# Order of three pairs of steps inside the second half of each group of tiles, in the layer stage of an AdaLN kernel

## The chip, the cores and the metric

One core of one Trainium2 chip runs the whole program. The metric is the time of one execution on the device in microseconds; the kernel before takes 2164.86 us (median of 3 runs, 2164.37 to 2165.76). The core has TensorE (PE in the rows; its weight loads are PEld), VectorE (DVE), ScalarE (ACT), GpSimd (POOL) and the queue SyncE (SP), which issues the DMAs. Each engine works through its own list of instructions in the order in which the program wrote them, and waits on semaphores.

## The reference

The input x has 4 sequences of 1024 tokens with 256 features. A small modulation network gives shift, scale and gate rows. First comes a normalised full attention with 4 heads, added to x through a gate. Then the input of the second part is normalised and modulated, goes through two layers, and is added through a second gate. One such layer is, cut to what matters here:

```python
h = shift_token(x)                       # half of the features come from the token before
q, k, v = split(h @ wqkv, 3)             # 8 heads of 64
q = l2norm(q) * qs;  k = l2norm(k) * ksc
q = q * cos * scale + rotate_half(q) * sin * scale      # k likewise, with 1/scale
o = local_attention(q, k, v)             # windows of 128 tokens: own one and the one before
x = x + o @ wo
h = layernorm(shift_token(x)) * lg + lb
a, g = split(h @ w1 + b1, 2)             # hidden size 682
x = x + (a * gelu(g)) @ w2 + b2
```

Everything is float32. Matrix products on TensorE are made of three products of rounded operands (hi*hi, hi*lo, lo*hi), so each operand has a "hi" copy, which ScalarE makes, and a "lo" remainder, which VectorE makes.

## The kernel before, in words

A set-up block and the first attention (`attention_block`) take about the first 700 us. The change is in `layers_block`, which handles both layers. It walks over 64 units of 128 tokens (32 a layer) in 16 groups of four (`QUAD`), g = 0 to 15, with a prologue g = -1. In group g, `first` is the group's first unit and `following` the first unit of the next group. Each engine has a hand-written list for a group, and the lists of all engines have the same skeleton.

First come 12 rounds r = 0 to 11 (`EARLY`) of attention: scores, softmax, transposes of the probabilities, value products. Then come 16 slots k = 0 to 15 (`SLOTS`). They hold the end of the attention; the q, k, v products of the group ahead (`qkv`, slots 0 to 11); the feed-forward part of the present group, 12 hidden units m = 0 to 11 of 114 or 113 features by 256 tokens; and the preparation of q and k of the group ahead. Six hidden units belong to one pair of token units. The text calls them unit 0 to unit 11.

What a hidden unit m passes through: `hidden` on PE in slot m + 4 makes the two products g and a in two of the banks A0 to A3. `gelu` (ACT L1420, slot m + 4) makes the gelu of g. `up_out` (DVE L1638, slot m + 5) multiplies it with a. `u_split` on ACT (L1427) makes the hi copy, `u_split` on DVE (L1644, slot m + 6) the lo remainder; its two inputs are both in SBUF. `outputs` on PE (L1281 to L1283, six matmuls) adds the unit to the layer's output in bank O or P; `outputs(0)` stands in slot 10, `outputs(5)` in slot 15, and units 6 to 11 follow in rounds 0 and 2 of the next group. `y_out` (DVE L1651) closes the six units of a pair.

What q and k of a unit n of the group ahead pass through: copies out of the bank to SBUF (ACT L1355); `squares` (ACT L1365); `sums` (DVE L1545); `trig`, three products with a table on POOL (two of L1802, one of L1807), which waits for the squares to have been summed; `norms` on DVE (lines 1551 to 1558 and `rsqrt`, 89 to 94); `rotated` (DVE L1563, L1565); `qk_transpose` on PE (L1210, eight transposes into the two banks T0 and T1); `qk_out` on ACT (L1372 for q, L1374 for k). There are only the banks T0 and T1 for these, so the transposes of the second unit wait until `qk_out` has emptied T0 of the first one's q. `sums` of the third unit is in slot 11 and of the fourth in slot 13, each with its `trig` on POOL one slot later.

`x_bias` (POOL L1820) adds the bias b2 to the residual, in slots 1, 5 and 7; its result is read by `y_out` at the end of the slots.

Of the kernel before, what the change touches and what calls it, by code (L numbers as in the profile page):

```python
# [1038 lines left out]
def layers_block(nc, io, scratch, out, ident, cols, share, early):  # L1039
# [3 lines left out]
    with ExitStack() as ctx:  # L1043
# [141 lines left out]
        def _(eng):  # L1185
# [68 lines left out]
            def x_transpose(n):  # L1254
                ps = fill(w, "x_t", n, "T")
                w.wait_ge(xn_ready, n + 1)
                for k in range(KC):
                    last = eng.transpose(ps[:, P * k:P * k + P], xn[:, n % 2, P * k:P * k + P], ident[:, :])
                last.then_inc(done["x_t"][0], 1)
# [27 lines left out]
            for g in range(-1, GROUPS + 1):  # L1287
                first, following, m0 = QUAD * g, QUAD * (g + 1), HC * g
                if g == GROUPS:
                    for j in range(NC):  # L1290
                        outputs(HC * (g - 1) + NC + j)
                    break
                if g >= 0:
                    for r in range(0, EARLY, 2):
                        if r >= 4:
                            p_transpose(*head(first, r - 4)), p_transpose(*head(first, r - 3))
                        scores(*head(first, r)), scores(*head(first, r + 1))
                        if g >= 1:
                            for j in OUT_AT.get(r, ()):
                                outputs(HC * (g - 1) + NC + j)  # L1300
                        elif r in (0, 2):
                            qkv(*LATE_V[r // 2])
                        if r in (4, 6):
                            qk_transpose(first + 2 + (r - 4) // 2)
                        if r == 8:
                            project(first)
                        if r == 10 and following < UNITS:
                            h_transpose(following)
                        if r >= 4:
                            values(*head(first, r - 4)), values(*head(first, r - 3))  # L1310
                for k in range(SLOTS):
                    ahead = following < UNITS
                    r = EARLY + 2 * k
                    if g >= 0 and k < 4:
                        p_transpose(*head(first, r - 4)), p_transpose(*head(first, r - 3))
                    if g >= 0 and k < 2:
                        scores(*head(first, r)), scores(*head(first, r + 1))
                    if k < HC and ahead and (following + k // 3, k % 3) not in LATE_V:
                        qkv(following + k // 3, k % 3)
                    if g >= 0:  # L1320
                        if k in (0, 4, 6):
                            project(first + (1, 0, 2, 3)[k // 2])
                        if k == 3:
                            x_transpose(first), x_transpose(first + 1)
                        if k == 0 and ahead:
                            h_transpose(following + 1)
                        if k < 4:
                            values(*head(first, r - 4)), values(*head(first, r - 3))
                    if k in (4, 7) and ahead:
                        h_transpose(following + 1 + k // 3)  # L1330
                    if k >= 4 and g >= 0:
                        hidden(m0 + k - 4)
                    if k == 9 and g >= 0:
                        x_transpose(first + 2), x_transpose(first + 3)
                    if k in (10, 11) and ahead:
                        qk_transpose(following + k - 10)
                    if k >= 10 and g >= 0:
                        outputs(m0 + k - 10)

        @block.scalar  # L1340
        def _(eng):
# [20 lines left out]
            def squares(n):  # L1362
                w.wait_ge(qk_ready, 2 * n + 2)
                w.wait_ge(t2_used, n - 1)
                eng.activation(t2[:, n % 2], qk[:, n % 3], ACT.Square).then_inc(sq_ready, 1)  # L1365
# [107 lines left out]
            for g in range(-1, GROUPS):  # L1473
                first, following, m0 = QUAD * g, QUAD * (g + 1), HC * g
                ahead = following < UNITS
                if g >= 0:
                    for r in range(EARLY):
                        if r == 8:
                            o_out(first)
                        if r >= 4 and r % 2 == 0:  # L1480
                            pt_out(*head(first, r - 4)), pt_out(*head(first, r - 3))
                        exps(*head(first, r))
                        if g == 0 and r in (1, 3):
                            qkv_out(*LATE_V[r // 2])
                        if r in (4, 6):
                            qk_out(first + 2 + (r - 4) // 2)
                        if r == 10 and ahead:
                            h_out(following)
                        if g == GL - 1:
                            for i in W_Q.get(r, ()):  # L1490
                                piece_q(i)
                        if g == GL:
                            for i in W_O.get(r, ()):
                                piece_o(i)
                            for i in W_1.get(r, ()):
                                piece_1(i)
                for k in range(SLOTS):
                    r = EARLY + 2 * k
                    if g >= 0:
                        if k in (0, 2, 4):  # L1500
                            o_out(first + 1 + k // 2)
                        if k < 4:
                            pt_out(*head(first, r - 4)), pt_out(*head(first, r - 3))
                    if k < HC and ahead and (following + k // 3, k % 3) not in LATE_V:
                        qkv_out(following + k // 3, k % 3)
                    if g >= 0:
                        if k < 2:
                            exps(*head(first, r)), exps(*head(first, r + 1))
                        if g == GL and k in (7, 9, 11):
                            piece_2((k - 7) // 2)  # L1510
                        if k == 3:
                            f_out(first), f_out(first + 1)
                    if (k in (4, 7) or k == 0 and g >= 0) and ahead:
                        h_out(following + 1 + k // 3)
                    if k in (2, 5, 10, 12) and ahead:
                        squares(following + k // 3 - k // 10)
                    if k >= 4 and g >= 0:
                        gelu(m0 + k - 4)
                    if k >= 5 and g >= 0:
                        u_split(m0 + k - 5)  # L1520
                    if k == 9 and g >= 0:
                        f_out(first + 2), f_out(first + 3)
                    if k in (11, 12) and ahead:
                        qk_out(following + k - 11)
                    if g == -1 and k == 3:
                        first_w2_wo()
                    if g == -1 and k == 6:
                        first_w1()
                if g >= 0:
                    u_split(m0 + HC - 1)  # L1530
# [250 lines left out]
        def _(eng):  # L1781
# [57 lines left out]
            def piece_2(i):  # L1839
                w.wait_ge(w2_hi, 2 + i + 1)  # L1840
                n = CS[2 * i]
                eng.tensor_tensor(w2[1][0:n, 2 * i:2 * i + 2, :].rearrange("p c n -> p (c n)"), AT_2[i][0:n, :],
                                  w2[0][0:n, 2 * i:2 * i + 2, :].rearrange("p c n -> p (c n)").bitcast(F32), ALU.subtract).then_inc(w2_ready, 1)
# [3 lines left out]
            for g in range(-1, GROUPS + 1):  # L1847
                first, following, m0 = QUAD * g, QUAD * (g + 1), HC * g
                ahead = following < UNITS
# [19 lines left out]
                for k in range(SLOTS):  # L1869
                    r = EARLY + 2 * k  # L1870
                    if k < 3 and g >= 0:
                        probabilities(*head(first, r - 2)), probabilities(*head(first, r - 1))
                    if g == GL and k in (7, 9, 11):
                        piece_2((k - 7) // 2)
                    if k in (1, 5, 7) and g >= 0:
                        x_bias(first + 1 + (k - 1) // 3)
                    if k in (4, 7, 12, 14) and ahead and (g >= 0 or k < 14):
                        trig(following + {4: 0, 7: 1, 12: 2, 14: 3}[k])
                if g >= 0:
                    finish(first), finish(first + 1)  # L1880

# [220 lines left out]
```

## Time and profile before

| | |
|---|---|
| median of 3 runs | 2164.86 us |
| the profiled execution's own time | 2162.62 us |
| its span | 2160.8 us |
| PE busy | 1869.9 us (87%) |
| PEld busy | 1395.4 us (65%) |
| DVE busy | 1529.1 us (71%) |
| ACT busy | 1186.4 us (55%) |
| POOL busy | 984.6 us (46%) |
| mean granted clock of TensorE | 0.953 |

The busy times overlap, and PE's is the time in which some matmul was in flight, not its speed. The 16 DMA engines were busy for about a tenth of the span. In the chain that ended last PE has 32% of the span, DVE 20% and ACT 8%. The layer stage begins at about 700 us. One group in the middle of it runs from 1170.22 to 1258.42 us, which is 88.2 us; the rows below are from this group unless they say otherwise.

### The profile page before, as it was taken

To read this page: it belongs to the slowest core of one execution; us is meant where nothing else is said; L and a number is where in the kernel's file an instruction comes from. 1 tells how busy PE (TensorE), PEld (TensorE's weight loads), DVE (VectorE), ACT (ScalarE), POOL (GpSimd) and SP (SyncE) were. 2 spreads that over 40 slices of the span, in tenths; PEclk is the share of its full clock that TensorE was granted. 3 is DMA by queue.
4 is the path that set the end of the run, shared out by engine and by line. 5 is a ranking of instruction groups with operands and counts; after the bars stand their busy time and mean duration, and the time that the engine had idled before them with its cause. 6 is when DMAs were issued, how large, how long until landed. Compare 5 with 4: busy or idle time off the path is not lost.

```text
span 2160.8 us, 36526 instructions
## 1 busy us (share of the span) xinstructions
PE 1869.9 (87%) x12941; PEld 1395.4 (65%) x12941; DVE 1529.1 (71%) x3736; ACT 1186.4 (55%) x2717; POOL 984.6 (46%) x781
## 2 busy tenths in 40 slices
PE   5568999999984899899999999888899998998996
PEld 3444444444443587777777877767787777877776
DVE  2668888676756686867867768586776867768674
ACT  0545545534343656656566565665656566565662
POOL 0324454647473545334444444543545445454451
PEclk7669999999996899999999999999999999999999
DMA  4000000101212000000000001111101000010100
GB/s 141 28 27 28 1 25 11 42 25 42 89 54 88 8 21 22 19 12 24 21 17 19 12 25 35 51 51 28 33 16 30 27 27 26 18 30 25 29 19 23
DMA packets 83407, 68.58 MB, mean 32 GB/s; under 512 B 10853, under 2 KB 79509, under 8 KB 83225
## 3 DMA queue, kind: packets, MB, share of 16 engines
q1 hardware_dynamic: 83224, 66.25, 9.9%
q8 instruction: 103, 1.69, 0.3%
q14 instruction: 80, 0.65, 0.1%
HBM read 45.22 MB, written 16.81 MB: 29 GB/s over the span
## 4 chain that ended last, share of the span: by engine, by line
PE 32%; DVE 20%; ACT 8%; issue 7%; DMA 1%; POOL 1%; DVEq 0%; ACTq 0%; SPq 0%; POOLq 0%
ACT share_x L1383 4%; PE bank_A L260 3%; PE bank_A L262 3%; PE bank_A L261 3%; PE bank_P L260 3%; PE bank_A L1220 3%; DVE l_t L1563 2%; PE bank_O L1243 2%; PE bank_P L262 2%; DVE share_x L1579 2%; PE bank_P L261 2%; PE bank_T L1231 2%; DVE l_u_lo L1644 2%; PE bank_T L1210 2%; PE bank_T L260 1%
## 5 line engine op out<-in xcount | busy, mean ns | idle before, releaser
L1814 POOL TENSOR_TENSOR share_x<-share_x,l_rinv 128x512 f32<-128x512 f32 (+1 forms) x256 | 249.9, 997 | 343.0 <-DVE l_rinv L1587 342.7
L1802 POOL TENSOR_TENSOR l_t<-share_qk,l_tab 128x512 f32<-128x512 f32 x128 | 176.0, 1396 | 318.7 <-DVE l_ss L1545 313.3
L1383 ACT ACTIVATE share_x<-share_x,l_nb 128x256 f32<-128x256 f32 (+1 forms) x512 | 248.2, 487 | 80.6 <-DVE l_nb L1579 80.4
L260 PE MATMUL bank_A<-l_f_hi,l_w_hi 128*114 128x256 f32 (+1 forms) x768 | 220.0, 286 | 6.2 <-DVE l_f_lo L1624 5.0
L262 PE MATMUL bank_A<-l_f_hi,l_w_lo 128*114 128x256 f32 (+1 forms) x768 | 216.1, 281 | 0.0
L261 PE MATMUL bank_A<-l_f_lo,l_w_hi 128*114 128x256 f32 (+1 forms) x768 | 215.9, 281 | 0.0
L1579 DVE CUSTOM_DVE_ANT_0 share_x<-bank_A,share_scr 128x256 f32<-128x256 f32 (+1 forms) x512 | 177.2, 401 | 42.7 <-PE bank_A L1220 42.5
L645 ACT ACTIVATE pr<-ps_S 128x1024 f32<-128x1024 f32 x128 | 130.6, 1022 | 124.7 <-PE ps_S L539 124.0
L1644 DVE TENSOR_TENSOR l_u_lo<-l_up,l_u_hi 114x256 fp32r<-114x256 f32 (+1 forms) x192 | 196.8, 1031 | 0.1
L1231 PE MATMUL bank_T<-ident,share_x 128*128 128x128 f32 x960 | 150.5, 287 | 53.1 <-POOL share_x L1814 40.1
L760 DVE TENSOR_REDUCE mxr<-ps_M 128x2 f32<-128x1024 f32 x128 | 154.9, 1210 | 36.3 <-PE ps_M L550 35.6
L895 POOL TENSOR_TENSOR acc<-acc,pr 128x1024 f32<-128x1024 f32 x64 | 156.2, 2441 | 53.0 <-ACT pr L645 48.7
L1231 PEld LDWEIGHTS bank_T<-ident,share_x 128*128 128x128 f32 x960 | 102.5, 142 | 95.8 <-issue 48.6
L1807 POOL TENSOR_TENSOR l_t<-share_qk,l_tab 128x1024 f32<-128x1024 f32 x64 | 157.7, 2464 | 0.0
L260 PE MATMUL bank_P<-l_wqkv_hi,l_h_hi 128*128 128x512 f32 x368 | 155.8, 423 | 1.5 <-ACT l_vt L1360 1.0
L1394 ACT COPY share_qk<-bank_T 128x512 f32<-128x512 f32 (+1 forms) x256 | 133.0, 557 | 42.9 <-PE bank_T L1231 40.9
L1420 ACT ACTIVATE share_x<-bank_A,cols 114x256 f32<-114x256 f32 (+1 forms) x192 | 90.8, 473 | 108.4 <-PE bank_A L262 101.9
L1355 ACT COPY share_qk<-bank_P 128x512 f32<-128x512 f32 x122 | 71.6, 587 | 141.7 <-PE bank_P L262 141.7
L1220 PE MATMUL bank_A<-l_kt,share_x 64*128 64x256 f32 (+1 forms) x1024 | 146.9, 403 | 0.7 <-DVE l_nb L1579 0.2
L1243 PE MATMUL bank_O<-share_qk,l_vt 128*64 128x128 f32 x1920 | 139.7, 283 | 8.0 <-DVE l_o_lo L1591 8.0
L261 PE MATMUL bank_P<-l_wqkv_lo,l_h_hi 128*128 128x512 f32 x368 | 146.3, 398 | 0.0
L260 PEld LDWEIGHTS bank_A<-l_f_hi,l_w_hi 128*114 128x114 f32 (+1 forms) x768 | 136.0, 177 | 15.7 <-issue 12.5
(269 smaller groups left out, 5098.8 us busy)
## 6 DMA issues: line engine op xcount, KB each, us to landing
l_xs<-x_layers SPq DMA_DIRECT2D x64, 128.0 KB, 2.5
share_x<-in_x SPq DMA_DIRECT2D x8, 512.0 KB, 3.8
base_rows<-share_x SPq DMA_DIRECT2D x16, 256.0 KB, 2.1
x_layers<-share_x SPq DMA_DIRECT2D x16, 256.0 KB, 2.1
l_xs<-x_layers SPq DMA_DIRECT2D x64, 64.0 KB, 2.1
x_layers<-l_yb SPq DMA_DIRECT2D x32, 128.0 KB, 1.8
share_m<-base_rows SPq DMA_DIRECT2D x32, 128.0 KB, 2.7
out<-l_yb SPq DMA_DIRECT2D x32, 128.0 KB, 1.7
```

What stands on the lines that cost most here:

```text
L260: pe.matmul(out, a_hi, b_hi, start=(start and k == 0), stop=False)
L261: pe.matmul(out, a_hi, b_lo, start=False, stop=False)
L262: last = pe.matmul(out, a_lo, b_hi, start=False, stop=(stop and k == n - 1))
L1220: last = eng.matmul(halves[e][:, 0:P * windows(n)], qt[rows, n % QUAD, c, :], kt[rows, key_slots(n), c, :], start=True, stop=True)
L1231: last = eng.transpose(ps[:, q:q + P], sm[:, R % SS, e, P * v:P * v + P], ident[:, :])
L1243: last = eng.matmul(banks["O"][HD * e:HD * e + HD, P * c:P * c + P], vt[:, s, q:q + HD], pt[:, R % 2, 2 * e + v, :], start=(v == 0), stop= ...
L1383: eng.activation(row, row, ACT.Exp, bias=nb[:, R % SS, e:e + 1], scale=-1.0, accum_out=rsum[:, R % SS, e:e + 1]).then_inc(ex_ready, 1)
L1579: eng.tensor_tensor_reduce(sm[:, R % SS, e, 0:P * windows(n)], ps[:, 0:P * windows(n)], keep, 1.0, 3.0e38, ALU.add, ALU.min, nb[:, R % SS, ...
L1644: eng.tensor_tensor(u_lo[0:CS[j], m % US, :], up[0:CS[j], m % 3, :], u_hi[0:CS[j], m % US, :].bitcast(F32), ALU.subtract).then_inc(u_ready, 1)
L1802: eng.tensor_tensor(dst[:, :, :, lo:lo + H2], src[:, :, :, hi:hi + H2], table[:, :, 1, lo:lo + H2].unsqueeze(2).to_broadcast([P, 2, LH, H2 ...
L1807: eng.tensor_tensor(t1[:, n % 2].rearrange("p (a h) d -> p a h d", a=2), src, table[:, :, 0, :].unsqueeze(2).to_broadcast([P, 2, LH, HD]), ...
L1814: eng.tensor_tensor(row, row, rinv[:, R % SS, :].unsqueeze(2).to_broadcast([P, 2, P * windows(n)]), ALU.mult).then_inc(pn_ready, 1)
```

## The change

Three edits, all in the slots. PE: in slots 10 and 11 `outputs(m0 + k - 10)` stands in front of `qk_transpose(following + k - 10)`, no longer behind it. ACT: in slots 11 and 12 `qk_out(following + k - 11)` stands in front of `gelu(m0 + k - 4)` and `u_split(m0 + k - 5)`. POOL: `trig` stands in front of `x_bias`; the two meet in slot 7 only, with `trig(following + 1)` and `x_bias(first + 3)`. DVE's and SP's lists are the same. No instruction is added or removed.

```diff
@@ PE
                     if k == 9 and g >= 0:
                         x_transpose(first + 2), x_transpose(first + 3)
+                    if k >= 10 and g >= 0:
+                        outputs(m0 + k - 10)
                     if k in (10, 11) and ahead:
                         qk_transpose(following + k - 10)
-                    if k >= 10 and g >= 0:
-                        outputs(m0 + k - 10)
@@ ACT
                     if k in (2, 5, 10, 12) and ahead:
                         squares(following + k // 3 - k // 10)
+                    if k in (11, 12) and ahead:
+                        qk_out(following + k - 11)
                     if k >= 4 and g >= 0:
                         gelu(m0 + k - 4)
                     if k >= 5 and g >= 0:
                         u_split(m0 + k - 5)
                     if k == 9 and g >= 0:
                         f_out(first + 2), f_out(first + 3)
-                    if k in (11, 12) and ahead:
-                        qk_out(following + k - 11)
@@ POOL
+                    if k in (4, 7, 12, 14) and ahead and (g >= 0 or k < 14):
+                        trig(following + {4: 0, 7: 1, 12: 2, 14: 3}[k])
                     if k in (1, 5, 7) and g >= 0:
                         x_bias(first + 1 + (k - 1) // 3)
-                    if k in (4, 7, 12, 14) and ahead and (g >= 0 or k < 14):
-                        trig(following + {4: 0, 7: 1, 12: 2, 14: 3}[k])
```

## Rows read from the trace of the kernel before

**Rows 1.** Busy time by engine between two moments: stretch, length, engines (instructions), clock, DMA.
```profile
1223.40:1245.47 22.07, 20.59 (x159) 18.93 (x160) 19.43 (x27) 11.11 (x24) 10.35 (x6) 1.00 0.00 1
```

**Rows 2.** Timeline of PE: start, length, instruction, count, idle time before and what ended it.
```profile
1227.95 1.09 PE L1210 MATMUL bank_T<-ident,l_t 128*128 128x128 f32 x8 [0.66 <-DVE l_t L1565]
1228.79 0.37 PE L1281 MATMUL bank_O<-l_w_hi,l_u_hi 114*128 114x256 f32 x1
...
1229.59 0.40 PE L260 MATMUL bank_P<-l_wqkv_hi,l_h_hi 128*128 128x512 f32 x1
...
1230.99 0.28 PE L260 MATMUL bank_A<-l_f_hi,l_w_hi 128*114 128x256 f32 x1
...
1233.21 1.15 PE L1210 MATMUL bank_T<-ident,l_t 128*128 128x128 f32 x8 [0.64 <-ACT share_x L1372]
1234.11 0.36 PE L1281 MATMUL bank_O<-l_w_hi,l_u_hi 114*128 114x256 f32 x1
...
1234.90 0.28 PE L260 MATMUL bank_A<-l_f_hi,l_w_hi 128*114 128x256 f32 x1
```

**Rows 3.** Timeline of ACT in the same slots.
```profile
1231.19 0.59 ACT L1360 COPY l_vt<-bank_P 128x512 f32<-128x512 f32 x1 [2.47 <-PE bank_P L262]
1231.91 0.47 ACT L1420 ACTIVATE share_x<-bank_A,cols 114x256 f32<-114x256 f32 x1
...
1232.57 0.59 ACT L1372 COPY share_x<-bank_T 128x512 f32<-128x512 f32 x1
...
1233.53 1.08 ACT L1365 ACTIVATE l_t<-share_qk 128x1024 f32<-128x1024 f32 x1
1235.81 0.48 ACT L1420 ACTIVATE share_x<-bank_A,cols 114x256 f32<-114x256 f32 x1 [1.20 <-PE bank_A L262]
```

**Rows 4.** Timeline of DVE, slots 8 to 15.
```profile
1217.24 2.25 DVE L1644 TENSOR_TENSOR l_u_lo<-l_up,l_u_hi 114x256 fp32r<-114x256 f32 x1
...
1220.07 0.18 DVE L1551 TENSOR_SCALAR l_ss<-l_ss 128x32 f32<-128x32 f32 x1
...
1232.79 0.47 DVE L1638 SCALAR_TENSOR_TENSOR l_up<-bank_A,cols,share_x 114x256 f32<-114x256 f32 x1
...
1236.52 0.48 DVE L1638 SCALAR_TENSOR_TENSOR l_up<-bank_A,cols,share_x 114x256 f32<-114x256 f32 x1 [1.93 <-PE bank_A L262]
1236.92 1.46 DVE L1644 TENSOR_TENSOR l_u_lo<-l_up,l_u_hi 114x256 fp32r<-114x256 f32 x1
...
1243.31 2.23 DVE L1644 TENSOR_TENSOR l_u_lo<-l_up,l_u_hi 113x256 fp32r<-113x256 f32 x2
1245.47 0.68 DVE L1651 TENSOR_TENSOR l_yb<-bank_O,l_yb 128x512 f32<-128x512 f32 x1
```

**Rows 5.** Timeline of POOL, slots 7 to 15.
```profile
1212.91 0.73 POOL L1820 TENSOR_TENSOR l_yb<-l_xs,share_scr 128x256 f32<-128x256 f32 x1 [4.16 <-DVE l_xs L1597]
1214.10 2.73 POOL L1802 TENSOR_TENSOR l_t<-share_qk,l_tab 128x512 f32<-128x512 f32 x2 [0.46 <-DVE l_ss L1545]
...
1233.01 2.73 POOL L1802 TENSOR_TENSOR l_t<-share_qk,l_tab 128x512 f32<-128x512 f32 x2 [13.81 <-DVE l_ss L1545]
1235.71 2.39 POOL L1807 TENSOR_TENSOR l_t<-share_qk,l_tab 128x1024 f32<-128x1024 f32 x1
1239.66 2.74 POOL L1802 TENSOR_TENSOR l_t<-share_qk,l_tab 128x512 f32<-128x512 f32 x2 [1.56 <-DVE l_ss L1545]
1242.36 2.56 POOL L1807 TENSOR_TENSOR l_t<-share_qk,l_tab 128x1024 f32<-128x1024 f32 x1
```

**Rows 6.** All instructions of line 1644: count, shortest, median and longest in ns.
```profile
L1644 DVE TENSOR_TENSOR l_u_lo<-l_up,l_u_hi x192: 407/1120/2248, 766.8 to 2149.5; 114x256 fp32r<-114x256 f32 x128, 113x256 fp32r<-113x256 f32 x64
```

**Rows 7.** Timeline of DVE in the first group of layer two.
```profile
1496.63 1.32 DVE L1554 TENSOR_SCALAR l_ss<-l_mv 128x2 f32<-128x2 f32 x1
```

**Rows 8.** Timeline of PE: the wait of slot 11 in groups 0 and 14.
```profile
788.36 0.82 PE L1210 MATMUL bank_T<-ident,l_t 128*128 128x128 f32 x5 [0.64 <-ACT share_x L1372]
...
2058.57 0.66 PE L1210 MATMUL bank_T<-ident,l_t 128*128 128x128 f32 x4 [0.64 <-ACT share_x L1372]
```

## The prediction

> **What bounds the kernel now.** I read the page first, then the chain of waits, then the timelines of all four engines over one group, because the page's shares are means over stages with different limits. PE is busy longest, but in the stretch that the change touches no engine is busy all the time: of 22.07 us PE has 20.59, DVE 19.43, ACT 11.11, POOL 10.35, at a granted clock of 1.00, the level of 2.4 GHz [rows 1]. So the question is who waits for whom. The reader is to see two holes on PE, 0.66 us ahead of the transposes of the first unit (they wait for DVE's `rotated`) and 0.64 us ahead of those of the second (they wait until ACT has emptied bank T0) [rows 2]. On DVE the hole is in front of unit 8: `up_out` starts at 1236.52 after 1.93 us idle, waiting for PE's product a [rows 4]. From the end of `norms` to there DVE goes almost without a pause, so what PE gains before counts only up to this hole. Behind it stands a second resource, which no view names as a releaser. DVE's `u_split` takes 0.41 us at its shortest and 1.12 at the median [rows 6]. The one of 1236.92 lasts 1.46 us and ends at 1238.38, just after POOL's L1807 ends at 1235.71 + 2.39 = 1238.10. The pair of 1243.31 ends at 1245.54, 0.62 after POOL's L1807 ends at 1242.36 + 2.56 = 1244.92, and `y_out` follows [rows 4, 5]. I read this as an exclusion: a `u_split` started during a POOL product waits for the end of that one instruction. POOL is delayed in turn by some 0.16 where DVE waits at a boundary (2.56 against 2.39) [rows 5]. Then the end of the group hangs on POOL: `y_out` comes when the fourth `trig` is over, this started at 1239.66, and it waited 1.56 us for `sums` [rows 5], which stands on DVE behind the `u_split` of 1236.92.
>
> The Trainium skill says the same in the page "SBUF — State Buffer", section "Who interferes with whom": a DVE instruction with two SBUF inputs and a GpSimd instruction that reads SBUF exclude each other, and the later one waits until the earlier is finished. The lengths of rows 4 to 6 agree. The rule speaks against a plain reading of this change: time won on PE in the slots is worth nothing unless it moves a boundary of POOL.
>
> **Edit 1, PE.** `outputs(0)` costs 1229.59 - 1228.79 = 0.80, of which about 0.1 is the slow first matmul behind transposes (0.37 against 0.28) [rows 2]; ahead of the transposes it costs 0.70. The hole of 0.66 is counted from the end of the last matmul in flight; a matmul of 0.28 takes its turn in 0.12, so the room is 0.82. It fits, the transposes stay at 1227.95, and what follows them starts 0.70 earlier: the v product is ready for ACT at 1231.19 - 0.70 = 1230.49, unit 7's `hidden` starts at 1230.99 - 0.70 = 1230.29. That takes 1.42 (1230.99 to 1233.21 - 0.64 - 0.16), then `outputs(1)` 0.70: PE is at the second transposes at 1232.41, against 1233.21.
>
> **Edit 2, ACT.** ACT's turns: two copies take 0.96 (1232.57 to 1233.53), one 0.48; `gelu` with the hi copy 0.66 (1231.91 to 1232.57); `squares` 0.96, estimated as its 1.08 less the 0.11 by which a copy of 0.59 outlasts its turn [rows 3]. New order: v copy 1230.49, `qk_out` of the first unit 1230.97, so T0 is free at about 1231.6, before PE asks; the second hole is gone. `gelu(7)` at 1231.93 instead of 1231.91 [rows 3], harmless, since DVE takes unit 7 at 1232.79 only [rows 4]. `squares` at 1232.59, second `qk_out` 1233.55, `gelu(8)` at 1234.51 instead of 1235.81. PE: second transposes 1232.41 to 1233.31 (0.90, rows 2), `hidden` of unit 8 at 1233.3 instead of 1234.90. In the trace `up_out` of unit 8 starts 1.62 after it (1236.52 - 1234.90), with the slow first matmul 1.70: 1235.0. After `gelu(8)` (0.48 and some 0.1 of signalling, an estimate) it is 1235.1. So `up_out` of unit 8 moves from 1236.52 to 1235.1, and `u_split` asks for its turn 0.40 later, at 1235.5.
>
> **The step that decides.** POOL's boundary between L1802 and L1807 is at 1235.71 [rows 5]. 1235.5 is before it by 0.2. The remainder then runs in the boundary, ends near 1236.0 instead of 1238.38, `sums` ends near 1237.2, and the fourth `trig` waits no more for it: it starts when the third ends, 1238.10 + 0.16 = 1238.27, instead of 1239.66. That is 1.39 us. `trig` itself lasts as long as before (5.26, from 1239.66 to 1244.92), DVE's last remainders and `y_out` follow it 1.39 earlier; PE, which is 1.6 ahead, isn't late. Everything in the next group starts from `y_out`, the scores' minima and POOL's release, so the gain should stay. `up_out` and PE find their banks free, as `up_out` runs two units ahead of the reuse.
>
> **Edit 3, POOL.** The `trig` of slot 7 starts no earlier: with `x_bias` done it still waits 0.46 for `sums` [rows 5]. `x_bias` moves from 1212.91, inside a wait of 4.16 for the residual, to behind L1807, at 1219.2; its reader `y_out` is 25 us away. Price: it holds the port while DVE is about to begin `norms`. With 0.73 + 0.16 it ends at 1220.1, `norms` starts at 1220.07 [rows 4]: 0.05. Below: 0, if such a small instruction isn't held up; against that, one of 128x2 elements took 1.32 under POOL's work [rows 7]. Above: 0.73, if `x_bias` gets its turn before the waiting `u_split` of 1217.24 [rows 4] and shifts the whole chain. I take 0.05, since at the boundary of 1238.10 and at that of 1244.92 the waiting DVE was next.
>
> **Sum.** Groups 0 to 14 have a group ahead. In 14 of them the timelines repeat within 0.05 us; the holes of groups 0 and 14 are again 0.64 [rows 8]. 14 x 1.39 = 19.5. Group 8, where layer two begins, has other spacings, with 0 to 1.4 possible; I take 0.7. `x_bias` gives back 15 x 0.05 = 0.8. In sum 19.4 us. The profiled execution took 2162.62 (span 2160.8), 2.2 under the median: it would come to 2143.2, the median from 2164.86 to 2145.5.
>
> **Rivals.** *The boundary is missed.* If `u_split` asks after 1235.71, it waits until 1238.10, as now, and `sums`, the fourth `trig` and `y_out` stay where they are; PE's 1.6 us end in a longer wait. For it speaks that the margin is 0.2 us at the end of a dozen steps; against it, that every step is a row of this group and that the groups don't scatter. It would hit all groups or none: 2164.86 + 0.8 = 2165.6, the change does nothing.
>
> *`x_bias` goes first, the boundary is met.* 15 x 0.73 = 11.0 us are paid, 20.2 won: 2155.7.
>
> *`x_bias` goes first, and nothing is won.* The mechanism is its port turn in front of the remainder of 1217.24; this pushes `norms`, the layer norm and `rotated` by 0.73 in each group. It decides as soon as the gain behind is under 0.73, so with a missed boundary: 2164.86 + 11.0 = 2175.9, slower.
>
> **Numbers.** Boundary met as forecast 0.62; met with the price of `x_bias` 0.10; missed 0.18; missed and paid 0.10. Less than 0.2% (4.3 us) can't be told from no change. So faster 0.72, same 0.18, slower 0.10. The first case alone would lie between 2142 (group 8 in full, no price) and 2149 (1.1 a group). The range goes from 2142 to 2167, which takes in the first three cases.
>
> **What would show it.** In the profile after: no idle ahead of the L1210 of slots 10 and 11 beyond 0.1 us; L1420 of unit 8 before the L1807 of the third `trig`, and the L1644 behind it under 0.6 us instead of 1.46; the fourth `trig`'s L1802 without a wait for L1545; `y_out` 1.4 us earlier counted from `norms`; L1820 of slot 7 directly behind L1807 and L1551 at most 0.1 later. The prediction is wrong if that L1644 still lasts over a microsecond up to the end of L1807, or if the shortened slots come back as a longer wait in the rounds of the next group.

## The result: 2140.32 us, and the profile after

The changed kernel takes 2140.32 us (median of 6 runs, 2139.02 to 2145.55), the kernel before, with three more runs beside it, 2162.61 (2157.89 to 2165.76). The ratio is 0.9904, 95% interval 0.9886 to 0.9922, which is 20.8 us (17 to 25); the two medians are 22.3 us apart. The direction, the size and the mechanism of the forecast (19.4 us) hold. The time itself lies 1.7 us under the range that was stated: the executions of either kernel fall into two clusters some 5 us apart, for which neither the sum nor its range had a term. Two executions of the kernel before that were taken beside experiments, of 2568.49 and 3446.82 us, are left out of every comparison as slow ones.

The page of the changed kernel, busy times and the chain:

```profile
span 2139.0 us, 36526 instructions
PE 1871.9 (88%) x12941; PEld 1400.3 (65%) x12941; DVE 1505.0 (70%) x3736; ACT 1185.0 (55%) x2717; POOL 989.3 (46%) x781
PE 34%; DVE 19%; issue 7%; ACT 7%; DMA 1%; POOL 1%; DVEq 0%; SPq 0%; ACTq 0%; POOLq 0%
```

The reader is to see DVE: the same 3736 instructions are busy 24.1 us less (1529.1 before). They don't do less, they are held up less: L1644 alone has 172.5 us in all instead of 196.8. This total is no measure of the gain, though. With the PE edit alone, which below gives the same time, L1644 has 182.8 us. PE is as busy as before, in a span 21.8 shorter.

The timelines show the same group as the rows of before (group 5). It is best counted from the group's last layer-norm statistics, DVE's L1602, at 1219.41 before and 1208.26 after, which is a shift of 11.15. First PE; this answers [rows 2]:

```profile
1216.00 0.28 PE L1281 MATMUL bank_O<-l_w_hi,l_u_hi 114*128 114x256 f32 x1
...
1216.80 1.09 PE L1210 MATMUL bank_T<-ident,l_t 128*128 128x128 f32 x8
1217.65 0.48 PE L260 MATMUL bank_P<-l_wqkv_hi,l_h_hi 128*128 128x512 f32 x1
...
1221.25 1.04 PE L1210 MATMUL bank_T<-ident,l_t 128*128 128x128 f32 x8
1222.05 0.36 PE L260 MATMUL bank_A<-l_f_hi,l_w_hi 128*114 128x256 f32 x1
```

Both holes are gone. The first transposes start where they did (8.54 after L1602 in both), the product behind them 0.8 earlier, unit 8's `hidden` (1222.05) 1.7 earlier. Then ACT, which answers [rows 3]:

```profile
1219.33 0.59 ACT L1360 COPY l_vt<-bank_P 128x512 f32<-128x512 f32 x1 [1.75 <-PE bank_P L262]
1219.82 0.59 ACT L1372 COPY share_x<-bank_T 128x512 f32<-128x512 f32 x1
...
1223.34 0.52 ACT L1420 ACTIVATE share_x<-bank_A,cols 114x256 f32<-114x256 f32 x1
```

`gelu(8)` stands 15.08 after L1602; 15.10 was forecast, and 16.40 was the kernel before. The stage that decides is on DVE and POOL, which answer [rows 4, 5]:

```profile
1222.04 1.41 DVE L1644 TENSOR_TENSOR l_u_lo<-l_up,l_u_hi 114x256 fp32r<-114x256 f32 x1
1223.95 0.48 DVE L1638 SCALAR_TENSOR_TENSOR l_up<-bank_A,cols,share_x 114x256 f32<-114x256 f32 x1 [0.50 <-PE bank_A L262]
1224.35 0.54 DVE L1644 TENSOR_TENSOR l_u_lo<-l_up,l_u_hi 114x256 fp32r<-114x256 f32 x1
1224.81 1.21 DVE L1545 TENSOR_REDUCE l_ss<-l_t 128x16 f32<-128x1024 f32 x1
...
1232.91 0.68 DVE L1651 TENSOR_TENSOR l_yb<-bank_O,l_yb 128x512 f32<-128x512 f32 x1
```

```profile
1208.02 0.92 POOL L1820 TENSOR_TENSOR l_yb<-l_xs,share_scr 128x256 f32<-128x256 f32 x1
1221.87 2.74 POOL L1802 TENSOR_TENSOR l_t<-share_qk,l_tab 128x512 f32<-128x512 f32 x2 [12.93 <-DVE l_ss L1545]
1224.57 2.58 POOL L1807 TENSOR_TENSOR l_t<-share_qk,l_tab 128x1024 f32<-128x1024 f32 x1
1227.12 2.92 POOL L1802 TENSOR_TENSOR l_t<-share_qk,l_tab 128x512 f32<-128x512 f32 x2
1229.98 2.39 POOL L1807 TENSOR_TENSOR l_t<-share_qk,l_tab 128x1024 f32<-128x1024 f32 x1
```

DVE's L1644 behind unit 8 starts at 1224.35, before POOL's boundary at 1224.57. It ends after 0.54 us instead of 1.46; POOL's L1807 takes 2.58 instead of 2.39 and shows the other side of the same meeting. The fourth `trig` has no wait for `sums` any more. `y_out` comes 24.65 after L1602 instead of 26.06: 1.41 us, against 1.39 forecast.

Where the difference sits in the whole program can be read from the first and last start of L1602, which runs four times a group (one row each, before and after):

```profile
L1602 DVE BATCH_NORM_STATS2 l_st<-l_xs x64: 412/427/430, 743.5 to 2129.0; 128x6 f32<-128x256 f32 x64
```

```profile
L1602 DVE BATCH_NORM_STATS2 l_st<-l_xs x64: 412/426/430, 739.5 to 2106.6; 128x6 f32<-128x256 f32 x64
```

Of the 22.4 us at the last start, 4.0 are there at the first already, ahead of the first changed step. Between them it is 18.4: this stage takes 1385.5 us before and 1367.1 after. Both parts are taken up below.

### The profile page after: what moved, and what is told of

Read it like the earlier page. It is cut to its first block, busy times and chain, and to the rows that moved or that the text cites. A ratio compares the mean times of both kernels' runs of the same rounds, so it can differ in the third digit from the quotient of the medians.

```text
span 2139.0 us, 36526 instructions
## 1 busy us (share of the span) xinstructions
PE 1871.9 (88%) x12941; PEld 1400.3 (65%) x12941; DVE 1505.0 (70%) x3736; ACT 1185.0 (55%) x2717; POOL 989.3 (46%) x781
## 4 chain that ended last, share of the span: by engine, by line
PE 34%; DVE 19%; issue 7%; ACT 7%; DMA 1%; POOL 1%; DVEq 0%; SPq 0%; ACTq 0%; POOLq 0%
ACT share_x L1383 4%; PE bank_A L260 4%; PE bank_A L262 3%; PE bank_A L261 3%; PE bank_P L260 3%; PE bank_A L1220 3%; PE bank_P L262 2%; PE bank_P L261 2%; DVE share_x L1579 2%; PE bank_O L1243 2%; DVE l_u_lo L1644 2%; PE bank_T L1231 2%; DVE l_t L1563 2%; PE bank_T L1210 2%; PE bank_T L260 1%
## 5 line engine op out<-in xcount | busy, mean ns | idle before, releaser
L1802 POOL TENSOR_TENSOR l_t<-share_qk,l_tab 128x512 f32<-128x512 f32 x128 | 178.8, 1419 | 351.8 <-DVE l_ss L1545 346.4
L895 POOL TENSOR_TENSOR acc<-acc,pr 128x1024 f32<-128x1024 f32 x64 | 156.1, 2439 | 48.2 <-ACT pr L645 43.7
L1644 DVE TENSOR_TENSOR l_u_lo<-l_up,l_u_hi 114x256 fp32r<-114x256 f32 (+1 forms) x192 | 172.5, 905 | 0.1
L1807 POOL TENSOR_TENSOR l_t<-share_qk,l_tab 128x1024 f32<-128x1024 f32 x64 | 157.5, 2461 | 0.0
L260 PEld LDWEIGHTS bank_A<-l_f_hi,l_w_hi 128*114 128x114 f32 (+1 forms) x768 | 136.2, 177 | 15.7 <-issue 12.5
L262 PE MATMUL bank_P<-l_wqkv_hi,l_h_lo 128*128 128x512 f32 x368 | 145.9, 397 | 0.0
```

The source lines that it names most:

```text
L260: pe.matmul(out, a_hi, b_hi, start=(start and k == 0), stop=False)
L262: last = pe.matmul(out, a_lo, b_hi, start=False, stop=(stop and k == n - 1))
L1644: eng.tensor_tensor(u_lo[0:CS[j], m % US, :], up[0:CS[j], m % 3, :], u_hi[0:CS[j], m % US, :].bitcast(F32), ALU.subtract).then_inc(u_ready, 1)
L1802: eng.tensor_tensor(dst[:, :, :, lo:lo + H2], src[:, :, :, hi:hi + H2], table[:, :, 1, lo:lo + H2].unsqueeze(2).to_broadcast([P, 2, LH, H2 ...
L1807: eng.tensor_tensor(t1[:, n % 2].rearrange("p (a h) d -> p a h d", a=2), src, table[:, :, 0, :].unsqueeze(2).to_broadcast([P, 2, LH, HD]), ...
```

## The experiments

**One edit at a time.** Each is the kernel before with one of the three hunks of the diff. PE alone:

```diff
+                    if k >= 10 and g >= 0:
+                        outputs(m0 + k - 10)
                     if k in (10, 11) and ahead:
                         qk_transpose(following + k - 10)
-                    if k >= 10 and g >= 0:
-                        outputs(m0 + k - 10)
```

> The kernel before with the PE edit alone (outputs in front of qk_transpose). Boundary theory: outputs(0) fills the first hole, v is ready 0.7 us earlier, gelu(7) comes at 1231.2 and qk_out behind it frees T0 at 1232.5, just when PE asks; unit 8's up_out at 1235.1, its u_split in POOL's boundary of 1235.7, and the group is 1.4 us shorter, nearly as with all three edits: 17 to 21 us faster in all, 2141 to 2146. Rival (all three edits are needed, each gives its part): about a third to a half, 7 to 11 us.

Measured: 2141.98 us, ratio to before 0.9898 (0.988 to 0.9916). That is the whole gain, to within what the runs tell, and the stage from first to last L1602 takes 1367.1 us, as with all three edits. In its timeline L1644 behind unit 8 again has 0.54 us, and POOL's boundary comes 0.22 us after its start:

```profile
1222.26 0.49 DVE L1638 SCALAR_TENSOR_TENSOR l_up<-bank_A,cols,share_x 114x256 f32<-114x256 f32 x1 [0.50 <-PE bank_A L262]
1222.66 0.54 DVE L1644 TENSOR_TENSOR l_u_lo<-l_up,l_u_hi 114x256 fp32r<-114x256 f32 x1
```

```profile
1222.88 2.58 POOL L1807 TENSOR_TENSOR l_t<-share_qk,l_tab 128x1024 f32<-128x1024 f32 x1
```

ACT alone, `qk_out` in front of `gelu` and `u_split`:

```diff
+                    if k in (11, 12) and ahead:
+                        qk_out(following + k - 11)
                     if k >= 4 and g >= 0:
                         gelu(m0 + k - 4)
...
-                    if k in (11, 12) and ahead:
-                        qk_out(following + k - 11)
```

> The kernel before with the ACT edit alone (qk_out in front of gelu and u_split). Boundary theory: the second hole of PE closes (hidden of unit 8 starts 0.76 us earlier), but up_out of unit 8 comes at 1235.8 and its u_split asks at 1236.2, after POOL's boundary of 1235.7; so it waits to 1238.1 as before and the time does not change: 0 to 2 us. Rival (time won on PE counts as such): 0.76 us in each of 14 groups, 10.6 us faster.

Measured: 2164.40 us, ratio 1.0006 (0.9996 to 1.0016). The hole of slot 11 closes and `up_out` of unit 8 comes 0.73 us earlier in the group, yet L1644 misses the boundary of 1235.90 and just waits longer:

```profile
1235.98 0.48 DVE L1638 SCALAR_TENSOR_TENSOR l_up<-bank_A,cols,share_x 114x256 f32<-114x256 f32 x1 [1.20 <-PE bank_A L262]
1236.38 2.20 DVE L1644 TENSOR_TENSOR l_u_lo<-l_up,l_u_hi 114x256 fp32r<-114x256 f32 x1
```

```profile
1233.19 2.74 POOL L1802 TENSOR_TENSOR l_t<-share_qk,l_tab 128x512 f32<-128x512 f32 x2 [13.81 <-DVE l_ss L1545]
1235.90 2.40 POOL L1807 TENSOR_TENSOR l_t<-share_qk,l_tab 128x1024 f32<-128x1024 f32 x1
```

Half of what the full change wins ahead of this `up_out` (0.73 us of 1.42) is worth nothing here. That refutes the rival by which PE time counts as such, and it is the missed boundary of the prediction's first rival, seen on the chip.

POOL alone:

```diff
+                    if k in (4, 7, 12, 14) and ahead and (g >= 0 or k < 14):
+                        trig(following + {4: 0, 7: 1, 12: 2, 14: 3}[k])
                     if k in (1, 5, 7) and g >= 0:
                         x_bias(first + 1 + (k - 1) // 3)
-                    if k in (4, 7, 12, 14) and ahead and (g >= 0 or k < 14):
-                        trig(following + {4: 0, 7: 1, 12: 2, 14: 3}[k])
```

> The kernel before with the POOL edit alone (trig in front of x_bias in slot 7). Boundary theory: x_bias sits behind the third product of trig and is over before norms starts: no change, within 1 us. Rival (x_bias holds up norms): up to 0.7 us in 15 groups, 11 us slower.

Measured: 2164.83 us, ratio 0.9995 (0.9984 to 1.0006). Nothing, in either direction. That speaks against both rivals of the prediction in which `x_bias` is paid for: each charges 11.0 us for this edit, and the interval allows 1.3 us of slowing at most.

**One instruction on either side of the boundary.** The sharpest test adds work to the changed kernel. In front of `u_split`:

```diff
+        idle = sb("idle", [P, 6])
...
+                    if k == 13 and ahead and g >= 0:
+                        eng.bn_stats(idle[:, :], b2[:, 0, :])
                     if k >= 6 and g >= 0:
                         u_split(m0 + k - 6)
```

> The changed kernel with one more instruction on DVE in each group: a bn_stats over constants (128x256, 0.41 us, result unused), in slot 13 between up_out of unit 8 and the u_split behind it. In the changed kernel that u_split starts 0.22 us before POOL's boundary (16.09 against 16.31, counted from the group's last L1602). Boundary theory: it now asks at 16.5, waits for L1807 to end at 18.7, sums and the fourth trig come 1.4 us later, and the whole gain of the change is lost in 14 groups: 20 us slower than the changed kernel, about 2160 to 2165. Rival (no exclusion, plain work on DVE): at most 0.4 us in 15 groups, 6 us, or nothing, since DVE has idle time there.

Measured: 2164.38 us, ratio to the kernel before 0.9995 (0.9984 to 1.0006). An instruction of 0.42 us has undone a gain of 20. L1645 here is L1644, one line further down. It starts at 1231.76, 0.14 us behind POOL's boundary of 1231.62:

```profile
1231.03 0.48 DVE L1639 SCALAR_TENSOR_TENSOR l_up<-bank_A,cols,share_x 114x256 f32<-114x256 f32 x1 [0.52 <-PE bank_A L262]
1231.43 0.42 DVE L1747 BATCH_NORM_STATS2 l_idle<-share_scr 128x6 f32<-128x256 f32 x1
1231.76 2.53 DVE L1645 TENSOR_TENSOR l_u_lo<-l_up,l_u_hi 114x256 fp32r<-114x256 f32 x1
```

```profile
1231.62 2.39 POOL L1810 TENSOR_TENSOR l_t<-share_qk,l_tab 128x1024 f32<-128x1024 f32 x1
1235.57 2.73 POOL L1805 TENSOR_TENSOR l_t<-share_qk,l_tab 128x512 f32<-128x512 f32 x2 [1.55 <-DVE l_ss L1546]
```

The lines L1805 and L1810 are the old L1802 and L1807, and the wait for `sums` is back (1.55). The same instruction behind `u_split`:

```diff
                     if k >= 6 and g >= 0:
                         u_split(m0 + k - 6)
+                    if k == 13 and ahead and g >= 0:
+                        eng.bn_stats(idle[:, :], b2[:, 0, :])
```

> The same additional bn_stats, but behind that u_split, in front of sums of the fourth unit. Boundary theory: u_split still gets the boundary, sums ends at 18.2 instead of 17.8 (counted from the group's last L1602), and POOL is busy until 18.86 anyway: nothing is lost, as fast as the changed kernel, 2139 to 2146. Rival (plain work): the same loss as with the instruction in front.

Measured: 2144.22 us, ratio to before 0.9907 (0.989 to 0.9924). It costs nothing that the four runs can tell from the changed kernel; a few us aren't excluded, since in its profiled execution the stage from first to last L1602 takes 1370.4 instead of 1367.1 (2.6 us of it in group 6, 1.3 in group 8, 1.2 less in group 14). The two kernels with the additional instruction have the same instructions and differ by 0.9%.

```profile
1227.88 0.51 DVE L1645 TENSOR_TENSOR l_u_lo<-l_up,l_u_hi 114x256 fp32r<-114x256 f32 x1
1228.32 0.41 DVE L1749 BATCH_NORM_STATS2 l_idle<-share_scr 128x6 f32<-128x256 f32 x1
```

```profile
1228.07 2.59 POOL L1810 TENSOR_TENSOR l_t<-share_qk,l_tab 128x1024 f32<-128x1024 f32 x1
```

**`sums` moved ahead, in the kernel before.** DVE's list alone, slot 13:

```diff
+                    if k == 13 and ahead and g >= 0:
+                        sums(following + 3)
                     if k >= 6 and g >= 0:
                         u_split(m0 + k - 6)
...
-                    if k in (3, 6, 11, 13) and ahead:
+                    if k in (3, 6, 11, 13) and ahead and (k < 13 or g < 0):
                         sums(following + k // 3 - 1)
```

> The kernel before, PE, ACT and POOL as they were; only DVE's list is changed: in slot 13 sums(following + 3) stands in front of u_split of unit 7. If the group hangs on the fourth trig waiting for sums behind a blocked u_split, this gives the same gain with the holes of PE still there: sums ends at 1238.0, trig starts at 1238.1 instead of 1239.66, 1.4 us in 14 groups, 18 to 22 us faster (unless the last hidden units of PE, which stay where they were, become the later side: up_out of unit 11 at 1242.9 still allows 1.4). Rival (the gain comes from the holes on PE): 0 to 2 us.

Measured: 2152.34 us, ratio 0.9946 (0.9931 to 0.9962): 11.7 us, a good half of what was expected. The direction tells that the fourth `trig` is on the path even with both holes of PE still there. The size was misjudged. With `trig` early and PE late, another `u_split` starts 0.15 us behind the boundary of the long product (L1809, the old L1807): it lasts 2.52 us, and unit 11's `up_out`, expected at 1242.9 in the time of the rows of before (23.50 after L1602), comes 24.20 after it. `y_out` waits for that and comes 25.48 after L1602, 0.58 us earlier than in the kernel before instead of 1.4.

```profile
1237.16 2.52 DVE L1644 TENSOR_TENSOR l_u_lo<-l_up,l_u_hi 114x256 fp32r<-114x256 f32 x1
1239.61 0.47 DVE L1638 SCALAR_TENSOR_TENSOR l_up<-bank_A,cols,share_x 113x256 f32<-113x256 f32 x1
```

```profile
1237.01 2.39 POOL L1809 TENSOR_TENSOR l_t<-share_qk,l_tab 128x1024 f32<-128x1024 f32 x1
```

**A version that beats both.** If blocked remainders hold up the group's end, they needn't stand there. The changed kernel, DVE's list:

```diff
                 if g >= 0:
                     up_out(m0 + HC - 1)
-                    u_split(m0 + HC - 2), u_split(m0 + HC - 1)
+                    if not ahead:
+                        u_split(m0 + HC - 2), u_split(m0 + HC - 1)
                     y_out(2 * g)
...  (rounds of the next group)
                         minima(*head(first, r))
+                        if r == 1 and g >= 1:
+                            u_split(m0 - 2), u_split(m0 - 1)
                         if r == 1:
                             norms(first // 2 + 1)
```

> The changed kernel with DVE's list changed at the group's end: y_out no longer waits behind the u_split of units 10 and 11, which stand blocked by the fourth trig for 1.8 us; they move behind the minima of rounds 0 and 1 of the next group, in front of norms. Theory: y_out starts at 22.6 to 22.7 instead of 24.65 (counted from the group's last L1602), the minima end before POOL's L1807 ends at 24.1, both remainders then take 0.75, and norms starts 1.2 to 1.4 us earlier: 15 x 1.3 = 18 to 20 us faster than the changed kernel, about 2120 to 2126. Rival: the outputs of units 10 and 11 on PE in round 2, or the clock of TensorE, take it back: 0 to 5 us.

Measured: 2128.15 us, ratio to the kernel before 0.9825 (0.9806 to 0.9845); with the changed kernel at 0.9904 that is some 17 us more, a little under the expected 18 to 20. `y_out` starts 22.60 after L1602, as expected. The remainders now take 0.76 together, after 2.44 in the changed kernel:

```profile
1228.79 0.69 DVE L1651 TENSOR_TENSOR l_yb<-bank_O,l_yb 128x512 f32<-128x512 f32 x1 [0.23 <-PE bank_O L1283]
...
1230.24 0.76 DVE L1644 TENSOR_TENSOR l_u_lo<-l_up,l_u_hi 113x256 fp32r<-113x256 f32 x2
```

The same two edits of DVE's list in the kernel before:

> The kernel before, PE, ACT and POOL as they were, with DVE's u_split of units 10 and 11 behind the minima of rounds 0 and 1 of the next group. Theory: y_out starts when outputs(5) is done (24.1 counted from the group's last L1602) instead of 26.05, the fourth trig ends at 25.5, while the minima run, and norms starts 1.2 to 1.4 us earlier: 14 to 19 us faster than the kernel before; the two gains are of different places and add up in the version that has both. Rival: the gain is there only with the change.

Measured: 2151.14 us, ratio 0.9941 (0.9923 to 0.9958), 12.8 us, slightly less than expected. The ratios 0.9904 and 0.9941 multiply to 0.9846, just above the interval of the version with both (0.9806 to 0.9845), but each has an interval of its own. So both gains are there without the other, which refutes the rival. Whether they only add up is not shown: with both it is about 4 us more than the sum, and the first group gets shorter by 1.16 us from the late remainders alone (89.79 to 88.63) and by 1.31 on top of the change (88.37 to 87.06).

**The level.** The changed kernel once more, unaltered:

> The changed kernel once more, unaltered, for the level. The first attention (up to about 770 us) took 4.0 us less in the profiled execution of the changed kernel than in that of the kernel before, though nothing there is changed. Theory: this is the scatter of single executions of every kernel of this case (2158 to 2166 for the kernel before, in two clusters), and the change is worth what the layer stage shows, 19 to 21 us between medians of many runs. Rival: the change moves the first part too, by some 4 us (code or data placement); then the difference between medians of many runs is 22 to 25 us.

Measured: 2142.86 us (2139.17 to 2148.21), ratio 0.991 (0.9894 to 0.9927), which is 19.5 us. The rival's 22 to 25 us are not there in the middle, though the interval (16 to 23) just reaches them. First and last L1602 in the profiled executions of this run, of PE alone and of ACT alone:

```profile
L1602 DVE BATCH_NORM_STATS2 l_st<-l_xs x64: 411/426/431, 739.5 to 2106.3; 128x6 f32<-128x256 f32 x64
```

```profile
L1602 DVE BATCH_NORM_STATS2 l_st<-l_xs x64: 412/427/430, 737.8 to 2104.9; 128x6 f32<-128x256 f32 x64
```

```profile
L1602 DVE BATCH_NORM_STATS2 l_st<-l_xs x64: 411/427/430, 743.8 to 2131.4; 128x6 f32<-128x256 f32 x64
```

The stage from first to last is 1366.8, 1367.1 and 1387.6. Where nothing is gained, in the kernel before, with ACT alone, with POOL alone and with the instruction in front of `u_split`, it is 1385.5 to 1387.6; the changed kernel and PE alone have 1366.8 to 1367.1. That is 18.4 to 20.8 us for the change.

None of the edits touches the first attention, and yet the executions of the kernel before and of the changed one fall into two clusters each, some 5 us apart. Of 47 of the kernel before (the six of the result and those taken beside the experiments) 17 lie between 2157.89 and 2161.65, with a median of 2160.03, and 30 between 2163.04 and 2168.60, with 2164.81. Of 12 of the changed kernel 7 lie between 2139.02 and 2140.76 (2139.45) and 5 between 2144.99 and 2148.21 (2145.46). Compared cluster by cluster the change is worth 20.6 and 19.4 us, which speaks against the rival. Whether the change makes the lower cluster more frequent (7 of 12 against 17 of 47) so few runs can't tell.

The traces say where the clusters part. The profiled executions of the changed kernel (both), of PE alone and with the instruction in front, all in the lower cluster, have their first L1602 at 737.8 to 739.5; the other seven at 742.4 to 744.1. Of the 4.0 us between before and after, 0.9 are there at 170 us and 3.4 at 186. In between stands the same kind of meeting: DVE's L822, a product with two inputs in SBUF, and POOL's L895, an addition. Before, L822 starts 1.25 us after POOL's addition and ends 0.55 behind the end of that; after, it starts 0.10 us ahead of it and takes 0.68 (before, then after):

```profile
172.53 1.65 DVE L822 TENSOR_TENSOR share_qk<-share_qk,cr 128x512 f32<-128x512 f32 x1
171.28 2.35 POOL L895 TENSOR_TENSOR acc<-pr 128x1024 f32<-128x1024 f32 x1 [23.45 <-ACT pr L645]
```

```profile
171.69 0.68 DVE L822 TENSOR_TENSOR share_qk<-share_qk,cr 128x512 f32<-128x512 f32 x1
171.79 2.82 POOL L895 TENSOR_TENSOR acc<-pr 128x1024 f32<-128x1024 f32 x1 [24.80 <-ACT pr L645]
```

This is read from traces and no run isolates it. What makes DVE come earlier there in some executions was not tried, and it can't be the whole story: the profiled execution with `sums` moved ahead has the short L822 as well and loses the time again later.

## Why the prediction was right in its steps and wrong in its time

- **The two holes and what follows on PE and ACT**: right. Transposes at 8.54 after L1602 (8.54 forecast), second transposes at 12.99 (13.00), `gelu(8)` 15.08 (15.10), `up_out` of unit 8 15.69 (15.7), `u_split` 16.09 (16.1).
- **The step that decides**: right, and shown by the instruction put on either side of the boundary. The margin turned out as 0.22 us; 0.2 was stated.
- **1.39 us in 14 groups**: 1.41 at `y_out` of group 5, and the L1644 behind unit 8 lasts 0.53 to 0.55 in all of the 14.
- **Edit 3**: 0.8 us were charged, nothing was paid. `x_bias` (0.92 with its wait) ends at 1208.94, L1551 starts at 1208.93 with 0.18 as before, and the next `up_out` stands 4.11 after L1602 in both kernels. DVE's waiting remainder was next at the boundary, as assumed; the run of the POOL edit alone shows the price of neither rival. The 0.8 us charged for nothing here and the 0.6 us counted too much for group 8 nearly cancel in the sum, which is luck.
- **Edit 2**: it was worked out together with edit 1, which left open whether it is needed. It isn't: PE alone gives as much. On its own it gives nothing.
- **Group 8**: 0.7 us was a guess, and it gave almost nothing: from its last L1602 to that of group 9 it is 99.48 before and 99.39 after. In the 8 us ahead of the first transposes the granted clock is 0.71 there, partly at the level of 1.2 GHz (a matmul of 0.41 instead of 0.28). No hole stands in front of these transposes, and the early `outputs` and `qk_out` push unit 7 back by 0.87 us. `up_out` of unit 8 comes only 0.58 us earlier, and the L1644 behind it misses POOL's boundary by 0.41:

```profile
1505.81 0.48 DVE L1638 SCALAR_TENSOR_TENSOR l_up<-bank_A,cols,share_x 114x256 f32<-114x256 f32 x1 [1.13 <-PE bank_A L262]
1506.21 2.28 DVE L1644 TENSOR_TENSOR l_u_lo<-l_up,l_u_hi 114x256 fp32r<-114x256 f32 x1
```

```profile
1505.80 2.41 POOL L1807 TENSOR_TENSOR l_t<-share_qk,l_tab 128x1024 f32<-128x1024 f32 x1
```

- **What failed: the last step of the sum, from the change to the time, and the width of the range.** The sum puts its 19.4 us on one level, "the median from 2164.86 to 2145.5", and gives the scatter of the executions no term. The level itself was a fair one: 41 later executions of the kernel before have a median of 2164.51. But it is the upper of two clusters, 2164.81 and 2160.03, and the three values of before (1.4 us apart) all lay in it. 2145.5 is then the upper cluster of the changed kernel (2145.46). Of the six executions of the result four lay in the lower one (2139.02 to 2140.76), and the median with them. Nothing on record told which cluster a median of six would fall into; that there are two was not seen. The range doesn't mend it: from 2164.86 the most favourable terms (14 x 1.39 + 1.4) give 2144.0, and the stated 2142 comes out only from the time of the profiled execution, 2162.62. The size of the change was 19.4 forecast against 20.8 and 19.5 measured.

Between the two profiled executions the layer stage differs by 18.4, not 19.7 (14 x 1.41). Most of what is missing lies in group 14, where the group's length falls by 0.36 instead of 1.4. The loss appears in the second of the two stretches below, the rounds of the next group (before, then after):

```profile
2069.40:2077.40 8.00, 6.56 (x50) 5.17 (x46) 7.59 (x28) 3.44 (x10) 4.39 (x6) 1.00 0.21 68
2077.40:2085.40 8.00, 7.03 (x50) 5.23 (x50) 7.93 (x21) 5.99 (x21) 3.49 (x4) 0.79 0.00 1
```

```profile
2045.90:2053.90 8.00, 6.44 (x48) 4.98 (x45) 7.59 (x28) 3.45 (x10) 4.40 (x6) 1.00 0.23 68
2053.90:2061.90 8.00, 7.03 (x38) 5.36 (x40) 7.93 (x21) 5.98 (x19) 3.50 (x4) 0.57 0.00 1
```

The granted clock, after a stretch in which PE is busy 6.44 of 8 us, drops to 0.57 of full speed over eight microseconds, against 0.79 before: more of the time at the level of 1.2 GHz. DVE then waits 0.97 us for the scores. The other traces show this as scatter on top of the change rather than a part of it. Group 14 takes 84.24, 85.68, 84.21 and 85.68 us in the four profiled executions in which nothing is gained (before, ACT alone, POOL alone, instruction in front), and 83.88, 82.82, 82.78 and 82.70 in four that have the gain (the changed kernel twice, PE alone, instruction behind). The pair above is a short one of the first kind and the longest of the second.

## What to carry to other kernels

Where VectorE and GpSimd work side by side on data in SBUF, ask for each two-input VectorE instruction which GpSimd instruction is running when it starts; here the one that started 0.22 us before a boundary took 0.54 us, and the one that started 0.14 us behind it took 2.53, the whole next product. The wait stands in no list of waits: it shows as one instruction with several lengths (L1644: 0.41 to 2.25 us for the same shape). It isn't confined to instructions with two inputs: in group 8 of the changed kernel this one, with a single input of two elements per partition, lasts until POOL's product of 1482.35 ends, where it takes 0.16 in group 5.

```profile
1482.34 2.40 DVE L1554 TENSOR_SCALAR l_ss<-l_mv 128x2 f32<-128x2 f32 x1
1482.35 2.37 POOL L1807 TENSOR_TENSOR l_t<-share_qk,l_tab 128x1024 f32<-128x1024 f32 x1
```

In a stage like this one, time won on the busiest engine counts only if it carries something over such an edge, and an instruction that would only wait for a product of GpSimd should not stand in front of the one that the next stage needs. For the stated time, look at how the single executions are spread, and give the range their scatter besides the sum's.

## What the runs showed of the hardware that was not expected

That the meeting of a VectorE instruction with the end of a GpSimd one acts as a switch: 0.42 us of harmless work in front of one instruction makes 20 us in the program, the same behind it nothing that could be told. That a statistics instruction with one SBUF input passes under GpSimd's products unhindered (0.42 at 1231.43 with POOL at work until 1231.62 and after it), while a two-input one of nearly the same size takes 2.53. And that the two clusters of the time, too, part where VectorE comes just before or just after the start of a GpSimd instruction, as far as two traces show it.
